# TensorE's chain and score signals: from the last matmul, or from a drain behind it

## What is computed

```python
# layer 0: deformable convolution and an MLP
xp = x @ w_in + b_in
h = gelu(batch_norm(depthwise_conv3x3(x)))
offset, mask = h @ w_off + b_off, softmax((h @ w_msk + b_msk).reshape(..., 4, 9))
y = dcn_core(xp, offset, mask) @ w_out + b_out      # 4 groups x 9 taps, each a bilinear sample of xp
x = x + gamma1 * layer_norm(y)
x = x + gamma2 * layer_norm(gelu(x @ w_fc1) @ w_fc2)
# layer 1: additive attention over the 3136 positions of an image, strictly causal
t = tokens(x); n = layer_norm(t)
scores = sum_a(tanh(f[:, i] + g[:, j] + b1) * w2)   # f, g = n @ W1, 16 wide
t = t + (exp(scores) * lower_triangle / its row sum) @ n
# then 64 experts, each on its 8 best positions of an image
t = t + expert_ffn(layer_norm(t))
```

## Time and profile before

| | |
|---|---|
| Median of three runs | 8978.42 us |
| Span of the profiled execution | 14670.7 us |
| PE busy | 7831.1 us |
| DVE busy | 6704.9 us |
| ACT busy | 6815.4 us |
| POOL busy | 6413.8 us |
| TensorE's mean granted clock | 0.744 |

### The profile page before, as it was taken

The page is one execution under the profiler, slowest core; times in us unless marked ns, Lnnn a source line. Parts: engine busy times, 40 slices in busy tenths (PEclk is TensorE's granted clock), DMA queues, the critical chain, the costliest instruction groups (busy, mean ns, idle before and its releaser), DMA issues.

```text
span 14670.7 us, 162317 instructions
## 1 busy us (share of the span) xinstructions
PE 7831.1 (53%) x48435; PEld 3785.6 (26%) x48435; DVE 6704.9 (46%) x19495; ACT 6815.4 (46%) x8248; POOL 6413.8 (44%) x6711
## 2 busy tenths in 40 slices
PE   4445655455555555555554555555555455444567
PEld 2122222222222222222222222222222222222234
DVE  4444434444444444444444444454444444344333
ACT  0234634455444554445444454444544355443465
POOL 4544444444444444444444444444444444444430
PEclk6667767777777777777777777777777777776778
DMA  2111111111111111111111111111111111222325
GB/s 64 41 50 39 36 38 39 46 41 38 37 41 49 36 40 38 42 49 34 40 37 46 45 34 39 38 48 44 37 39 35 51 40 37 55 62 63 107 58 162
DMA packets 559311, 703.51 MB, mean 48 GB/s; under 512 B 256976, under 2 KB 371536, under 8 KB 556288
## 3 DMA queue, kind: packets, MB, share of 16 engines
q0 software_dynamic: 214624, 439.98, 11.0%
q1 hardware_dynamic: 343808, 252.97, 6.1%
HBM read 579.54 MB, written 112.84 MB: 47 GB/s over the span
## 4 chain that ended last, share of the span: by engine, by line
another core or an unknown queue 37%; ACT 17%; DVE 16%; issue 13%; PE 12%; DVEq 5%; DMA 1%; SPq 0%; ACTq 0%
ACT tanh L1882 14%; PE score_ps L2072 5%; DVEq L1347 5%; DVE pool_mem L1564 2%; PE side_ps L2012 1%; DVE y L1573 1%; PE value_ps L2101 1%; PE side_ps L1982 1%; DVE expoT L1641 1%; ACT L1892 1%; DVE pool_mem L1551 1%; PE turn_ps L1951 1%; ACT L1867 1%; ACT expo L1892 1%
## 5 line engine op out<-in xcount | busy, mean ns | idle before, releaser
L1882 ACT ACTIVATE tanh<-key_rep,query 128x896 f32<-128x896 f32 (+7 forms) x6400 | 5565.3, 951 | 4618.0 <-remote 2987.3
L1328 POOL DMA_INDIRECT pool_mem<-patches_odd,pool_mem x3375 | 3226.1, 956 | 4002.7 <-DVE y L1573 2977.5
L1328 POOL DMA_INDIRECT pool_mem<-patches_even,pool_mem x3332 | 3187.6, 957 | 3857.4 <-DVE y L1573 2815.5
L2072 PE MATMUL score_ps<-tanh,score_w 128*32 128x512 f32 (+3 forms) x24320 | 3461.1, 604 | 1933.9 <-ACT tanh L1882 1057.1
L2072 PEld LDWEIGHTS score_ps<-tanh,score_w 128*32 128x32 f32 x24320 | 826.2, 120 | 3979.9 <-issue 2624.8
L2101 PE MATMUL value_ps<-values,expoT 128*128 128x129 f32 (+1 forms) x5200 | 908.4, 317 | 408.3 <-issue 329.7
L1564 DVE TENSOR_TENSOR pool_mem<-pool_mem 128x384 f32<-128x384 f32 (+1 forms) x2352 | 1089.1, 532 | 12.9 <-issue 7.6
L1573 DVE TENSOR_REDUCE y<-pool_mem 128x64 f32<-128x2304 f32 x392 | 999.1, 2549 | 31.9 <-issue 9.6
L2012 PE MATMUL side_ps<-near_map,hatT 112*64 112x480 f32 x2792 | 806.3, 685 | 318.6 <-DVEq L1347 206.0
L2101 PEld LDWEIGHTS value_ps<-values,expoT 128*128 128x128 f32 (+1 forms) x5200 | 790.6, 223 | 524.8 <-issue 399.8
L1892 ACT ACTIVATE expo<-score_ps,tiny 128x896 f32<-128x896 f32 (+9 forms) x416 | 383.4, 922 | 1017.1 <-remote 743.1
(11 more groups left out here) (194 smaller groups left out, 8060.3 us busy)
## 6 DMA issues: line engine op xcount, KB each, us to landing
pool_mem<-in_weight SPq DMA_DIRECT2D x64, 1024.0 KB, 9.3
pool_mem<-patches_odd,pool_mem POOLq DMA_INDIRECT x3375
pool_mem<-patches_even,pool_mem POOLq DMA_INDIRECT x3332
patches_even<-pool_mem SPq DMA_DIRECT2D x104, 256.0 KB, 2.0
patches_odd<-pool_mem SPq DMA_DIRECT2D x104, 256.0 KB
pool_mem<-in_x SPq DMA_DIRECT2D x56, 224.0 KB
x_tok<-in_x SPq DMA_DIRECT2D x192, 64.0 KB
x_d<-x SPq DMA_DIRECT2D x192, 64.0 KB
```

The costliest lines, as they stand in the source:

```text
L1328: pool.indirect_dma_start(gathered[:, b, j * 4 * CG:(j + 1) * 4 * CG], None, patches_flat[int(odd)], bass.IndirectOffsetOnAxis(ap=index[:, ...
L1882: nc.scalar.activation(tanh[:, TANH_AT[ui][0]:TANH_AT[ui][1]], key_rep[:, lo:lo + w], ACT.Tanh, bias=query[:, col:col + 1]).then_inc(tanh_ ...
L2072: last = mm(score_ps[32 * col:32 * col + 32, ci % 2, lo:hi], score_w[:, place], tanh[:, TANH_AT[ui][0] + lo:TANH_AT[ui][0] + hi], start=pl ...
```

## The change

In the seven chain steps and in `score`, the increment is taken from the last matmul and put on a drain of PE that is issued behind it. The other PE steps, the `values` steps with their turns and the side bank's steps among them, keep their increments on matmuls. The order of the steps on every engine, and what each waits for, is as it was.

```diff
@@ task of the PE block
-                    last.then_inc(y_turned.sem, 1)
+                    nc.tensor.drain().then_inc(y_turned.sem, 1)
...
-                    last.then_inc(mixed.sem, 1)
+                    nc.tensor.drain().then_inc(mixed.sem, 1)
...
-                    turn(chain_ps[:, :r], mid[:r], r).then_inc(mid_turned.sem, 1)
+                    turn(chain_ps[:, :r], mid[:r], r)
+                    nc.tensor.drain().then_inc(mid_turned.sem, 1)
...
-                    last.then_inc(hid_done.sem, 1)
+                    nc.tensor.drain().then_inc(hid_done.sem, 1)
...
-                    last.then_inc(mlp_done.sem, 1)
+                    nc.tensor.drain().then_inc(mlp_done.sem, 1)
...
-                    turn(chain_ps[:, :r], values[:r, value_place(odd, i), :C], r).then_inc(norm_turned.sem, 1)
+                    turn(chain_ps[:, :r], values[:r, value_place(odd, i), :C], r)
+                    nc.tensor.drain().then_inc(norm_turned.sem, 1)
...
-                    mm(chain_ps[:, P:P + r], w_q[:].rearrange("p a b -> p (a b)"), chainT[:, :r], start=True, stop=True)\
-                        .then_inc(keys_done.sem, 1)
+                    mm(chain_ps[:, P:P + r], w_q[:].rearrange("p a b -> p (a b)"), chainT[:, :r], start=True, stop=True)
+                    nc.tensor.drain().then_inc(keys_done.sem, 1)
...
-                    last.then_inc(scored.sem, 1)
+                    nc.tensor.drain().then_inc(scored.sem, 1)
```

## The result

The changed kernel takes 8992.97 us (median of 16 runs, 8988.45 to 9004.5), the kernel before 8979.31 us (16 runs). The ratio is 1.0018, 95% interval 1.0011 to 1.0025: slower by some 14 us. The forecast was 9070 us, a loss of 92. The time lies in the stated range, but the loss is less than a sixth of the one forecast, and what happened is the first rival, "hidden by the gathers", which had 0.22 and gave 8990 us. The prediction was wrong.

The account below looks back on a forecast made before the run. The prediction took POOL's gathers to pace the middle, with PE, DVE and ACT close under them: 8978 us, plus 80 in the middle and 12 behind the last gather, gave 9070 us, range 8975 to 9400 us.

Parts of the forecast that it names:

- the first rival: Whole kernel: the margin of PE, DVE and ACT under the gathers exceeds what they lose; 8990 us, chance 0.22.
- the 80 us of the middle: First to last gather: growth forecast because PE, DVE and ACT become slower than POOL; 87 us, of which 80 kept.
- the group's new pace: Middle, PE, DVE and ACT with the drains: 8200 + 308 = 8508 us.
- POOL's need: Middle: time POOL needs for 6707 gathers at 1.256 us each, 8421 us.
- I take half: Middle: PE, DVE and ACT together pass on half of PE's real delay of 617 us, 308 us.
- Own pace: Middle: time PE, DVE and ACT would take by themselves before the change, 8200 us, between 7560 and 8508.
- The margin: Middle: PE, DVE and ACT lie under POOL by 8421 - 8200 = 221 us, between 0 and 861.
- The end: Behind the last gather: 47 score and about 17 chain steps with drains add 15 us, of which 12 count.
- The price of a drain: PE: 0.35 us behind a chain step, 0.20 us behind a score step, together 823 us.
- The group already sets the pace: Middle: PE, DVE and ACT have no margin and pass on most of the loss; 9300 to 9450 us, chance 0.24.
- The drain does nothing: PE: its stream isn't held, or only until the same event as before; 8978 us, chance 0.07.
- Faster: Score steps: the drain keeps PE's next step off, so ACT's tanh gets its signal sooner; 8936 us, chance 0.05.

Follow-up runs that it names:

- e1: The kernel before with 5 gathers left out of every sub-block, the work of PE, DVE and ACT kept: 8590.86 us.
- e6: The changed kernel with a second lot of drains, one behind every other PE step, all gathers kept: 9145.33 us, ratio 1.0182.
- e2: The changed kernel with 5 gathers left out of every sub-block, the work of PE, DVE and ACT kept: 8740.44 us.
- e5: The kernel before with 5 gathers left out of every sub-block and drains in the score steps only: 8619.78 us.
- e0: The kernel before, unchanged, run again for a second profile: 8976.89 us.
- e9: The changed kernel without the drains near and behind the last gather, all the others kept: 8985.34 us, ratio 1.0008.
- e8: The kernel before with drains only in steps near and behind the last gather: 8986.38 us, ratio 1.0008.

## Why the prediction was wrong

The account of who sets the pace was the right one. The step that failed is the comparison that made the 80 us of the middle: the group's new pace against POOL's need. The forecast had the group overrun POOL by 87 us; the runs have it short of POOL by 265 us. Two terms of it were mis-sized, POOL's need and the "I take half". Either one at its measured size, with the rest as I had it, would have hidden the drains and given the 8990 us of the first rival. A third fault is in the working itself.

- **POOL's need.** I had 1.256 us a gather, 8421 us. In the unstretched profile of the kernel before it is 8544 us, 1.274 us a gather. Two thirds of the 123 us that were missing stood in my own rows: I multiplied the median, 944 ns, by the count, where the earlier trace rows have 6413.44 us for 6707 gathers, a mean of 956 ns. With the mean the need is 8503 us. The other 41 us come with the stretched profile; in the unstretched one the median is the same and the mean 969 ns. The 87 us that I took for POOL's waits in a timed run were slower gathers; there are 1.5 us of waits.
- **What the group passes on.** I took half of 617 us, 308, with no row for the half. Measured is 150 us, a quarter of 617, the very share that I named for "a partner stands idle" and passed over. As the price of a drain was higher than mine (below), the true share is smaller still.
- **The comparison.** The group's new pace of 8508 us is just what I had the middle take already (8978 - 73.5 - 397 = 8508). By my own numbers the middle need not have grown at all; to add 80 us I set 8508 against POOL's 8421 and added the difference to a time that already held it. The sentence on POOL's 87 us of waits touches on this and takes off only 7 us for it.
- **Own pace.** 8200 us; e1's middle is 8116 us. That is near, but by luck in part: it was a pick between 7560 and 8508, and the pieces themselves gave 8686. The bounds held. The granted clock was 1.00 in 12 of the 29 pieces, not in most of them as I wrote; the sum uses no clock.
- **The margin** that follows was 221 us and is 428, as far as e1 tells; the loss to be set against it was 308 and is 150 to 163.
- **The end.** 12 us forecast; 10 in the profiles, 7 in the runs. Right. Some 6 us ahead of the last gather were not forecast by the rival that came true, and stay open.
- **The price of a drain.** I had the next start moved by 0.15 us behind a score step (0.20 in the sum) and by 0.24 us behind a chain step, with 0.11 us more for the stopped array. The traces have 0.32 and 0.36 us for the move alone. The term of 0.08 us from the end to the next start, taken from DVE, is what was too small: it is 0.25 us on average. The 0.11 us were not measured apart. The sum lacked the sequencer's own instructions that a drain brings into the open. A drain costs PE more than I thought, and the kernel lost less: the price was not what made the forecast too high.
- **The other rivals.** "The group already sets the pace" (9300 to 9450 us) is refuted by e1; e6 shows it at 9145 us once the own pace has been raised to it. "The drain does nothing" is refuted by e2. The 9900 us that stand there for all 823 us are a slip; the sum is 9813. "Faster" (8936 us) is refuted where it could be seen: e5, with drains behind the score steps alone, is slower than e1 by 29 us, and ACT's `tanh` waits longer for scores in e2 than in e1 (lines below).

Of the Trainium skill: "PSUM — Partial Sum Buffer", section "Engine vs sequencer instructions", has a drain wait for a fully idle engine, and the trace agrees (in the rows above the step behind a drain starts 0.11 and 0.33 us after the last matmul's end). The estimate of 163 ns a drain from "TensorE: Matmul & The Clock Gate", sections "Single matmul latency" and "Back-to-back issue gap", led to the 8990 us of the rival. It came near the measured time because a low price makes the loss fit the margin, and that is luck: 163 ns is half of what the traces have, 0.32 and 0.36 us a drain.

What ACT waited for scores, in e1 and then in e2 (where the score drain is L2077):

```profile
ACT tanh L1883 <- PE score_ps L2073: 469.3, 214, 8.2
```
```profile
ACT tanh L1883 <- PEq L2077: 534.0, 248, 7.4
```

In the whole kernels, where the gathers pace, the same wait hardly moves: e0, then the changed kernel (where the score drain is L2076).

```profile
ACT tanh L1882 <- PE score_ps L2072: 634.3, 239, 33.0
```
```profile
ACT tanh L1882 <- PEq L2076: 620.4, 243, 30.6
```

## What to carry to other kernels

Where one engine paces the kernel, the question for a cost on the others isn't its size but the margin, and that is measured by taking work from the pacing engine: two runs, with and without the change, gave both the margin (428 us, perhaps somewhat less with all gathers there) and the cost (150 us). Costs below the margin nearly vanish: 14 us of 150 were left, half of them behind the paced part. Costs can't be added up from single measurements either, 55 and 29 us made 150, and once the margin is used up they show: the second lot brought the kernel from 8993 to 9145 us. And a count is multiplied by a mean, not by a median: here that alone moved POOL's need by 82 us.

In this kernel a drain on TensorE cost PE the overlap with the next step and the sequencer's work for that step's waits, 0.32 to 0.36 us together, and gained nothing, so here the signal belongs on the last matmul.

## What was not expected of the hardware

- A profile can be stretched by 63% (14670.7 us for a run of 8979 us) while a later one of the same kernel isn't (8975.1 us). In the stretched one POOL "waits" 5793 us, in the other 1.5 us. Instructions' medians agree (a gather 944 ns in both), means not quite, waits not at all.
- Drain costs aren't additive: 55 and 29 us alone, 150 us together, and 517 us with another lot behind other steps.
- What a drain costs PE depends on what its sequencer has to do for the next step. Where nothing of the sequencer stands between, the next matmul starts 0.08 us (chain, 102 cases) or 0.11 us (score, 359) behind the end; with one register instruction between 0.21 or 0.24 us; with a register instruction and a semaphore wait 0.32 or 0.36 us (medians, changed kernel).
- With the drains the mean granted clock of TensorE is higher: 0.904 to 0.908 in the 16 runs of the changed kernel, 0.892 to 0.898 in the runs of the kernel before that stand beside the experiments; e9, with nearly all drains, has 0.905 to 0.908, e8, with 66, 0.893 to 0.897. I had costed no change. In e1 and e2 it doesn't rise (0.916 to 0.920 and 0.914 to 0.918), so it isn't what the 150 us hinge on. The cause is not shown.
